# Entry of a two-layer decoder kernel: a barrier of all engines replaced by one wait per input, with constants and transfers in the order of their first use

## The reference

```python
def _L0_attn_ref(x, time_decay, time_mix_k, ..., W_r, W_k, W_v, W_g, W_o, ln_gamma, ln_beta):
    xx = jnp.concatenate([x[:, 1:2, :], x[:, :-1, :]], axis=1) - x
    xk = x + xx * time_mix_k
    xv = x + xx * time_mix_v
    xr = x + xx * time_mix_r
    xg = x + xx * time_mix_g
    r = xr @ W_r.T
    k = xk @ W_k.T
    v = xv @ W_v.T
    g = jax.nn.sigmoid(xg @ W_g.T)
    w = jnp.exp(-jnp.exp(time_decay))
    attn = _rwkv_scan(r, k, v, w)
    y = attn * g @ W_o.T
    ...
x = _layernorm(x + _L0_attn_ref(x, ...))
x = _layernorm(x + _L0_xattn_ref(x, ctx_1024, ctx_1024, mask, 1, ...))
x = _layernorm(x + _L0_ffn_ref(x, ...))
x = _layernorm(x + _L1_attn_ref(x, ...))
x = _layernorm(x + _L1_xattn_ref(x, ctx_1024, ctx_1024, ...))
x = _layernorm(x + _L1_ffn_ref(x, ...))
```

## Time and profile before

| what | value |
|---|---|
| median of three runs | 1245.17 us (1242.21 to 1247.08) |
| the profiled execution, its time | 1248.9 us |
| the same, span from first to last instruction | 1247.2 us |
| mean granted TensorE clock over the span | 0.969 of full speed |
| PE busy | 1156.8 us (93%), 8404 matmuls |
| DVE, ACT, POOL busy | 828.3, 646.6, 152.1 us |

### The profile page before, as it was taken

How to read it: one execution, slowest core, us unless ns; L and a number is a source line. 1 busy time by engine, 2 the same in 40 slices (tenths; PEclk the granted TensorE clock), 3 DMA queues, 4 the chain that set the end, 5 groups by cost and what they waited for, 6 DMA issues and landing times.

```text
span 1247.2 us, 22856 instructions
## 1 busy us (share of the span) xinstructions
PE 1156.8 (93%) x8404; PEld 958.7 (77%) x8404; DVE 828.3 (66%) x2630; ACT 646.6 (52%) x1363; POOL 152.1 (12%) x184
## 2 busy tenths in 40 slices
PE   3899999889999989999989999988999999999996
PEld 2667888767888867888877788876787878888875
DVE  5634557773657872565875565687788778696663
ACT  2236542325644225654224754276667876958562
POOL 4799404100000000000000000000001000000000
PEclk9999999999999999799999999998989899998988
DMA  8200000100000100000010101120000100001000
GB/s 310 105 18 1 1 1 1 51 18 1 2 2 1 45 25 1 2 1 1 1 35 18 71 2 43 43 68 1 1 18 9 27 13 23 1 27 35 18 10 17
DMA packets 21388, 33.27 MB, mean 27 GB/s; under 512 B 11424, under 2 KB 12192, under 8 KB 20128
## 3 DMA queue, kind: packets, MB, share of 16 engines
q1 hardware_dynamic: 21280, 31.82, 7.5%
HBM read 27.62 MB, written 4.19 MB: 26 GB/s over the span
## 4 chain that ended last, share of the span: by engine, by line
PE 75%; DVE 15%; ACT 6%; issue 2%; POOL 1%; ACTq 0%; DVEq 0%; POOLq 0%
PE ps L506 40%; PE ps L756 6%; PE ps L654 4%; DVE z L1617 2%; PE ps L646 2%; PE ps L644 2%; PE ps L672 2%; PE ps L671 2%; DVE arena L1811 2%; DVE arena L1431 2%; PE ps L670 2%; ACT L1288 1%; PE ps L610 1%; PE ps L701 1%; PE ps L905 1%
## 5 line engine op out<-in xcount | busy, mean ns | idle before, releaser
L506 PE MATMUL ps<-wts,arena 128*128 128x256 f32 (+2 forms) x1008 | 199.8, 354 | 17.9 <-DVE pq L1461 6.5
L506 PE MATMUL ps<-arena,wts 128*128 128x256 f16 (+1 forms) x1344 | 183.0, 289 | 20.6 <-ACTq L479 20.6
L506 PEld LDWEIGHTS ps<-wts,arena 128*128 128x128 f32 (+1 forms) x1008 | 152.2, 153 | 55.7 <-DVE pq L1461 7.5
L506 PEld LDWEIGHTS ps<-arena,wts 128*128 128x128 f16 (+1 forms) x1344 | 150.0, 112 | 46.5 <-issue 20.5
L1617 DVE SCALAR_TENSOR_TENSOR z<-ps,small,z 128x256 f32<-128x256 f32 x256 | 123.9, 484 | 41.3 <-PE ps L756 26.8
L756 PE MATMUL ps<-wts,pq 128*128 128x256 f32 x512 | 120.8, 380 | 6.2 <-DVE z L1617 6.2
L1222 ACT ACTIVATE pq<-ps 128x512 f32<-128x512 f32 x72 | 43.0, 597 | 144.9 <-PE ps L506 144.5
L1502 DVE CUSTOM_DVE_ANT_0 pq<-ps,mb 128x128 f32<-128x128 f32 x128 | 36.8, 287 | 114.0 <-PE ps L646 113.3
L756 PEld LDWEIGHTS ps<-wts,pq 128*128 128x128 f32 x512 | 92.6, 190 | 18.7 <-DVE z L1617 4.9
L1094 ACT ACTIVATE arena<-ps 128x512 f32<-128x512 f32 (+2 forms) x112 | 63.8, 580 | 64.0 <-PE ps L506 47.8
L1288 ACT ACT_TABLE_LOAD x70 | 89.8, 1283 | 1.2
(11 more groups left out here) (286 smaller groups left out, 2375.4 us busy)
## 6 DMA issues: line engine op xcount, KB each, us to landing
cT<-in_cT SPq DMA_DIRECT2D x16, 256.0 KB, 2.7
wts<-in_up SPq DMA_DIRECT2D x1, 2304.0 KB, 15.4
wts<-in_down SPq DMA_DIRECT2D x1, 2304.0 KB, 20.4
xT<-in_xT SPq DMA_DIRECT2D x8, 256.0 KB, 3.7
xin<-in_x SPq DMA_DIRECT2D x8, 256.0 KB, 3.0
xmid<-xin SPq DMA_DIRECT2D x8, 256.0 KB, 2.0
wts<-in_w SPq DMA_DIRECT2D x2, 1024.0 KB, 5.1
wts<-in_c SPq DMA_DIRECT2D x16, 128.0 KB, 3.1
```

The lines of the kernel that those rows point to most:

```text
L506: ins = mm(out_, l, r, start=(n == 0), stop=(n == len(pairs) - 1))
```

## The change

Every call of `done`, `loaded` and `gate` goes. PE waits, in turn 0 alone, for each mixed input and its weight, and later for the mark of each group of weights and constants; DVE and ACT likewise. POOL makes the constants in the order in which they are used, in two groups that end in the marks `shapes` and `rows`, and takes over the clearing of `V`, `zrow` and `c3` from DVE. SP issues its DMAs in another order, and waits for none of them.

```diff
@@ tensor
-                colproj(s, "rT", wr, r["xr"], [], 0, 2)
-                colproj(s, "vT", wv, r["xv"], [], 0, 2)
-                rowproj(s, "k", wk, r["xk"], [])
-                colproj(s, "g", wg, r["xg"], [], 0, 2)
+                def entering(i, w):
+                    return [("mixed", s, i), (w,)] if pe.turn == 0 else []
+                colproj(s, "rT", wr, r["xr"], entering(0, "W_r"), 0, 2)
+                colproj(s, "vT", wv, r["xv"], entering(1, "W_v"), 0, 2)
+                rowproj(s, "k", wk, r["xk"], entering(2, "W_k"))
+                colproj(s, "g", wg, r["xg"], entering(3, "W_g"), 0, 2)
...
-            done(pe, 0)
-            loaded(pe, 0)
-            gate(pe, 0)
...
+                    if f == rwkv_tokens and g == 0:
+                        eng.wait_ge(*pe.at("shapes"))
...
+                        if g == 0:
+                            eng.wait_ge(*pe.at("W_o"))
                         rowproj(0, "y", wo, carve_r(0)["ag"], [("ag", 0)])
...
+                        eng.wait_ge(*pe.at("wqo"))
                         colproj(s, "Q", wq, zT[s], [("zT1", s, "out")], m0, m1, b=b)
...
-                        eng.wait_ge(*pe.at("rest"))
+                        eng.wait_ge(*pe.at("wkv"))
+                        eng.wait_ge(*pe.at("rows"))
                         colproj(s, "K", wkk, cT[s], [("cT", s)], 0, AM)
@@ scalar
-            eng.wait_ge(*act.at("lam"))
+            eng.wait_ge(*act.at("columns"))
+            eng.wait_ge(*act.at("tdma"))
             A(t1, t1, ACT.Exp).then_inc(*act.up())
...
-                A(toT[:, k, :], ramp, ACT.Exp, scale=lamT[:, k:k + 1]).then_inc(*act.up())
+                A(toT[:, k, :], ramp, ACT.Exp, scale=lamT[:, k:k + 1]).then_inc(
+                    *act.up("powers" if k == KC - 1 else None))
             nc.scalar.preload_act_table_set("natural_log_exp_and_others")
-            done(act, 0)
-            loaded(act, 0)
...
-            gate(act, 0)
+            eng.wait_ge(*act.at("shapes"))
@@ vector
             v.stage("ready")
-            for s in range(NS):
-                V = carve_a(s)[0][2]
-                V_.memset(V, 1.0).then_inc(*v.up())
-            V_.memset(zrow[:, :], 0.0).then_inc(*v.up())
             V_.memset(tick[:, :], 0.0).then_inc(*v.up())
-            for s in range(NS):
-                V_.memset(c3[s][:, :], 0.0).then_inc(*v.up())
-            V_.memset(t1e[:, :, :], 0.0).then_inc(*v.up())
...
-            eng.wait_ge(v.sem("first_x"), 16 * (NS + 1))
             for s in range(NS):
+                eng.wait_ge(*v.at("first", s))
                 mixes(s)
                 v.mark(("mixed_x", s))
-            eng.wait_ge(*v.at("t1"))
+            V_.memset(t1e[:, :, :], 0.0).then_inc(*v.up())
+            eng.wait_ge(*v.at("powers"))
...
-            done(v, 0)
-            loaded(v, 0)
-            gate(v, 0)
+            eng.wait_ge(*v.own())
+            eng.wait_ge(*v.at("shapes"))
...
+                if g == 0:
+                    eng.wait_ge(*v.at("rows"))
+                    eng.wait_ge(*v.at("W_o"))
@@ gpsimd: what is made up to the mark shapes, in this order
+            iota pint, iota ramp, memset eps x3, hcol, ident, le
+            copy pcol[0], copy ramp, select hcol, select ident
+            tensor_scalar pcol[1], pcol[2], pcol[3] -> mark "columns"
+            select hcol, select le x2
             hmask: copy and three adds, twice (as before)
+            memset onesq -> mark "shapes"
@@ gpsimd: and behind it
+            memset qneg, sbig, srow, onesb, zrow, then c3 and V of each sequence
+            select qneg, sbig x2, copy identb, select srow x3
+            copy srow[0] -> mark "rows"
@@ sync
-            for s in range(NS):
-                dma(xT[s][:, :, :], a["xT"][B - NS + s], "first_x")
-            dma(mix[:, :, :], a["mixes"], "first_x")
-            dma(lamT[:, :], a["decay_cols"], "tdecay")
-            dma(t1, a["time_decay"].unsqueeze(0).to_broadcast([P, C]), "tdecay", "tdma")
...
+            dma(mix[:, :, :], a["mixes"], "first_x0")
+            dma(xT[0][:, :, :], a["xT"][B - NS], "first_x0", ("first", 0))
+            dma(wr, a["W_r"], "first_r", "W_r")
+            dma(t1, a["time_decay"].unsqueeze(0).to_broadcast([P, C]), "tdecay")
+            dma(lamT[:, :], a["decay_cols"], "tdecay", "tdma")
+            dma(xT[1][:, :, :], a["xT"][B - NS + 1], "first_x1", ("first", 1))
+            for d, s_ in ((wv, "W_v"), (wk, "W_k"), (wg, "W_g")):
+                dma(d, a[s_], f"first_{s_}", s_)
             for d, s_ in ((gam, "gamma"), (bet, "beta"), (bo_, "bo")):
                 dma(d, a[s_].unsqueeze(0).to_broadcast([P, C]), "weights0")
-            eng.wait_ge(*sp.own())
-            eng.wait_ge(sp.sem("tdecay"), 32)
-            done(sp, 0)
...
+            dma(wo, a["W_o"], "weights0", "W_o")
...
+            for d, s_ in ((wkk, "Wk"), (wvv, "Wv")):
+                dma(d, a[s_], "weights_kv", "wkv" if s_ == "Wv" else None)
             inputs(0, False)
             inputs(0, True)
+            for d, s_ in ((wq, "Wq"), (woo, "Wo")):
+                dma(d, a[s_], "weights_qo", "wqo" if s_ == "Wo" else None)
+            for d, s_ in ((rw, "router"), (up, "up"), (down, "down")):
+                dma(d, a[s_], "weights_rest", "rest" if s_ == "down" else None)
```

More of the change, by code:

```diff
@@ L465, in lane @@
             return Lane(nc, eng, who, book, sems, ctx)
[L467 to L479, removed]
         @block.tensor
@@ L719, in router @@
                 eng.wait_ge(*pe.at("zT2r", s))
+                if pe.turn == 0:
+                    eng.wait_ge(*pe.at("rest"))
                 o = take(("route", s), ("route", s, "out"), b)
@@ L1169, in _ @@
                 act.stage("attn")
+                if g == 0:
+                    eng.wait_ge(*act.at("rows"))
                 ups = UPS if g else 1.0
@@ L1431, in mixes @@
                         V_.scalar_tensor_tensor(dst[:, k, :], xx[:, k, :], mix[:, i, k:k + 1], x[:, k, :],
-                                                  ALU.mult, ALU.add).then_inc(*v.up())
+                                                  ALU.mult, ALU.add).then_inc(
+                            *v.up(("mixed", s, i) if v.turn is None and k == KC - 1 else None))
             def rwkv_evict(s):
@@ L2046, in _ @@
             po.stage("consts")
[L2047 to L2054, removed]
+            sel = G.affine_select
@@ L2055, in _ @@
+            G.iota(pint[:, :], [[0, 1]], base=0, channel_multiplier=1).then_inc(*po.up())
+            G.iota(pq[:, C + T:C + 2 * T].bitcast(I32), [[0, TT], [-1, P]], base=MID, channel_multiplier=0).then_inc(*po.up())
             for i, e in enumerate((LN_EPS, ML_EPS, 1.0)):
                 G.memset(eps[:, i:i + 1], e).then_inc(*po.up())
-            G.iota(pint[:, :], [[0, 1]], base=0, channel_multiplier=1).then_inc(*po.up())
-            G.iota(pq[:, C + T:C + 2 * T].bitcast(I32), [[0, TT], [-1, P]], base=MID, channel_multiplier=0).then_inc(*po.up())
+            G.memset(hcol[:, :], 1.0).then_inc(*po.up())
@@ L2059, in _ @@
+            G.memset(ident[:, :], 0.0).then_inc(*po.up())
+            G.memset(le[:, :], 1.0).then_inc(*po.up())
             eng.wait_ge(*po.own())
-            sel = G.affine_select
+            G.tensor_copy(pcol[:, 0:1], pint[:, :]).then_inc(*po.up())
+            G.tensor_copy(ramp, pq[:, C + T:C + 2 * T].bitcast(I32)).then_inc(*po.up())
+            sel(out=hcol[:, :], in_=hcol[:, :], compare_op=ALU.is_ge, fill=0.0, base=0,
+                   pattern=[[-RD, 8]], channel_multiplier=1).then_inc(*po.up())
@@ L2061, in _ @@
             sel(out=ident[:, :], in_=ident[:, :], compare_op=ALU.not_equal, fill=1.0, base=0,
                    pattern=[[-1, P]], channel_multiplier=1).then_inc(*po.up())
+            eng.wait_ge(*po.own())
+            G.tensor_scalar(pcol[:, 1:2], pcol[:, 0:1], float(-MID), None, ALU.add).then_inc(*po.up())
+            G.tensor_scalar(pcol[:, 2:3], pcol[:, 0:1], float(-P - MID), None, ALU.add).then_inc(*po.up())
+            G.tensor_scalar(pcol[:, 3:4], pcol[:, 0:1], -1.0, float(MID), ALU.mult, ALU.add).then_inc(*po.up("columns"))
@@ L2063, in _ @@
+            sel(out=hcol[:, :], in_=hcol[:, :], compare_op=ALU.is_ge, fill=0.0, base=RD - 1,
+                   pattern=[[RD, 8]], channel_multiplier=-1).then_inc(*po.up())
             for c in (0, T):
@@ L2065, in _ @@
                        pattern=[[1, P]], channel_multiplier=-1).then_inc(*po.up())
[L2066 to L2087, removed]
             eng.wait_ge(*po.own())
@@ L2098, in _ @@
             po.stage("ready")
[L2099 to L2102, removed]
+            G.memset(onesq[:, :], 1.0).then_inc(*po.up("shapes"))
+            G.memset(qneg[:, :], 0.0).then_inc(*po.up())
+            G.memset(sbig[:, :], 0.0).then_inc(*po.up())
+            G.memset(srow[:, :, :], 0.0).then_inc(*po.up())
+            G.memset(onesb[:, :], 1.0).then_inc(*po.up())
+            G.memset(zrow[:, :], 0.0).then_inc(*po.up())
```

(30 more changed lines are left out.)

## The result

Over 17 runs each, interleaved, the changed kernel takes **1239.95 us** (median) and the kernel before 1251.42; the ratio is **0.9923, interval 0.9901 to 0.9944**, so it is faster by 0.6 to 1.0%. That is 9.6 us of 1250 (the medians differ by 11.5, the means by 10.2), where 14.0 were forecast, and 1239.95 lies above the range of 1228 to 1236.5. The direction was right, the size not. The profiled execution comes out at the 1234.9 of the working: 1234.96 us with a span of 1233.2, against 1248.9 and 1247.2.

The account below looks back on a forecast made before the run. The entry barrier, with ACT its last member, was taken to hold PE's first matmul until 20.55 us; starting at 6.5 saves 14.0, so the median goes from 1245.2 to 1231.2 us, range 1228 to 1236.5.

Parts of the forecast that it names:

- The start of PE: Entry: PE's first matmul comes at 6.5 us instead of 20.55, once the first mixed input and W_r are there.
- the two landings given: Entry: W_r, issued at 2.0, lands at 4.9 if it takes xT's 2.9, at 6.4 if its old 4.4.
- The bound of 8.1 from contention: Entry: four DVE instructions each waiting for a short POOL one add 1.6 us, so PE starts at 8.1.
- PE runs through: Eight projections: the 64 matmul rows still take 15.46 us without a stall; ACT begins evicting r at 11.8.
- Nothing behind it is late: Behind the projections: POOL's second group done at 23, first wanted at 43; `down` lands at about 33; no cost.
- The sum: Whole kernel: 20.55 - 6.5 = 14.0 us off, profiled execution 1234.9, median 1231.2.
- the base and the clock it stood for: Whole kernel: the 14.0 us are subtracted from a median of 1245.2 us, giving 1231.2.
- rival D: Whole program: shifted against the TensorE clock grants, 45 us more at the lower level give 1251, slower; chance 0.03.
- Rivals A: Entry: DVE or W_r late by contention, PE starts at 8.1 to 9, 1233 to 1234 us; chance 0.08.
- B: Projections: PE halts at the seventh's bank behind DVE or late `powers`; gain 6 to 9, 1236 to 1239; chance 0.06.
- C: Entry: transfers are what is late, first matmul beyond 14, nothing gained, 1239 to 1245 us; chance 0.03.

Follow-up runs that it names:

- old_pool: Changed kernel with POOL's constants in the old order and DVE's clearing back in front of the mixes; ratio 0.9925, 1239.4 us at equal clock.
- pe_wo: Changed kernel with PE also waiting for the second mixed input and weight W_o before its first matmul; ratio 0.9948, 1242.5 us at equal clock.
- pe_wkv: Changed kernel with PE's first matmul also waiting for the second mixed input, W_o and cross attention's Wv; ratio 0.9983, 1247.2 us at equal clock.
- gate_new: Changed kernel with the entry barrier put back, new orders of constants and transfers kept; ratio 0.997, 1248.5 us at equal clock.
- old_sp: Changed kernel with the DMAs in the old order, SP's wait for the first group included; ratio 0.9907, 1238.8 us at equal clock.

## Why the prediction was wrong, point by point

- **The start of PE: right.** Forecast 6.5, measured 5.99. xT[0] landed at 4.2 instead of 4.4, and W_r at 5.0 (issued at 1.98, 3.0 to land), near the lower of the two landings given, 4.9 and 6.4; 6.5 had stood close to the upper. The bound of 8.1 from contention did not occur. Contention is real, but the working had its price on the wrong engine. DVE is held up by the long selects (old_pool), which the change moves away. Beside the short instructions DVE keeps its pace; POOL's copy took 0.70 when DVE had begun 0.05 before it, and 0.19 when it began 0.05 before DVE.
- **PE runs through: right.** 15.70 for the 64 rows against 15.46, no wait in between, ACT evicting r at 11.82 (forecast 11.8).
- **Nothing behind it is late: right, with one wrong size.** POOL's second group was done at 18.6, not 23: it began at 7.8 (about 9 assumed), its memsets took 6.1 (8 assumed; clearing V took 1.83 each, not 2.2), and the selects and the cast 4.8 (6 assumed). `down` landed at 38.0 instead of 33, so 2 later than the 36 of before and not 3 earlier. The queue moved 275 and 361 GB/s from 5 to 10 and from 10 to 15 us, where 419 had been assumed early, and the context and input loads now stand ahead of `down`. Both had cover enough, and no wait on the chain names them.
- **The sum: right at equal clock, in part by luck.** 14.0 forecast, 14.0 (1250.4 - 1236.4) found. But the start moved by 14.56, and each microsecond of it gave 0.96; the two small errors cancel. In the profiles the head of turn 1 moved by 15.7, as one slow output projection fell away, and 1.7 were lost behind it.
- **The step that failed is the base and the clock it stood for.** The three runs shown, with a median of 1245.17, lay low: 79 later runs average 1250.0. I subtracted from 1245.17 and took the clock as unchanged. That these three runs had a high clock is likely, but no clock of theirs is on record. The forecast of 1231.2 is thus 4.8 low by its base, and 3.8 by the term that I had set at zero, the lower granted clock of the changed kernel. Those two make 8.6 of the 8.75 between 1231.2 and 1239.95. I had rival D at 0.03, and only as a case that ends slower. Its mechanism came in part, at about a quarter of the size it needed (0.0039 of the mean clock is some 10 us more at the lower level, against the 45 of the prediction), and at nearly the price given: 0.45 forecast per microsecond at the lower level, and 9.8 per 0.01 of mean clock is 0.40 (0.01 of 1245 us is 12.5, twice that at half speed is 25, and 9.8/25). It belonged in the range: the spread from run to run should have been read as a spread of the clock, with the median of three runs uncertain by some 5 and not 3 (my estimate: single runs of the kernel before scatter with a standard deviation of 3.9 us).
- **Rivals A, B and C fell** with the chain: the first matmul came at 5.99, PE is nowhere idle in the projections, and xT[0] had landed by 4.2 and W_r by 5.0.

Open: why the mean clock of the changed kernel is 0.0039 lower over 33 runs against 79, more than four standard errors. The draws of it were 0.9620, 0.9620 and 0.9662, the last 0.9636 with the run of 1250.47 us. pe_wo, pe_wkv and gate_new, which start latest of the variants, have 0.9659, 0.9659 and 0.9682, which would fit an effect of the early start, but old_sp, which starts at 8.83, has 0.9663 (error 0.0017). No experiment here separates an effect of the early start from one of where the program's idle stretches fall.

## What to carry to other kernels

A barrier at the entry costs the distance between its last member and the first two tiles that the critical engine needs; here 12.1 of the 14.0 us. Cut it per input, and then order constants and transfers by first use: this is worth 2 to 3 us each, measured one at a time, once the barrier is gone, and 1.9 together while it stands. When a kernel keeps TensorE over 90% busy, compare versions at equal granted clock as well as by medians, and take a base from many runs: the entry's gain was 14.0 at equal clock and 10 in the means.

## What the runs showed of the hardware that was not expected

The time of one program varies by some 14 us from run to run (1241.71 to 1255.9 in 35 runs of the kernel before), and the mean granted clock accounts for most of it, at 9.8 us per 0.01: in all 79 runs the standard deviation is 3.9 us, and 1.3 about the line. Which of DVE and POOL pays when both read SBUF went with which began first, by as little as 0.05 us. POOL's small instructions ran faster in the changed entry: the cast into `pcol` took 0.19 (0.43 before), and that of the identity 0.30 where the earlier trace rows has 1.16. The order of the constants decides it, not the barrier: old_pool has 0.43 and 1.16 again, and gate_new 0.19 and 0.29. In the old order DVE's L1431 and subtractions run beside both casts, so contention would explain it; no run was made to show that.
